# Self-attention on one core: order of the reciprocals, of the next norm's work and of the negated maxima

## Chip, core, metric

One core of a Trainium2 chip runs the whole program; seven cores are idle. The metric is the device time of one execution in microseconds (us). A core has TensorE (PE, matrix products into PSUM), VectorE (DVE), ScalarE (ACT), GpSimd (POOL, which reads and writes SBUF only) and SyncE (SP, which issues the DMAs). Each engine works through its own instructions in the order in which they are written and waits on semaphores for the others.

## The reference, cut to what matters

x is (8, 512, 256), the context (8, 64, 192), all float32. Two blocks follow each other: a cross-attention block (16 heads of 16, then a feed-forward), and a block of three parts. The first of these three is the self-attention that the change touches:

```python
def _ln(x, g, b):
    m = jnp.mean(x, axis=-1, keepdims=True)
    v = jnp.var(x, axis=-1, keepdims=True)
    return (x - m) * jax.lax.rsqrt(v + EPS) * g + b

# HEADS = 16, D_HEAD = 64, N = S = 512
q = (xq @ Wq).reshape(B, N, HEADS, D_HEAD)
k = (xc @ Wk).reshape(B, S, HEADS, D_HEAD)
v = (xc @ Wv).reshape(B, S, HEADS, D_HEAD)
attn = softmax(einsum('bnhd,bshd->bhns', q, k) * D_HEAD ** -0.5)
out = einsum('bhns,bshd->bnhd', attn, v).reshape(B, N, HEADS * D_HEAD)
return out @ Wo + bo

x = _attn(_ln(x, g1, b1), _ln(x, g1, b1), Wq1, Wk1, Wv1, Wo1, bo1) + x   # changed here
x = _attn(_ln(x, g2, b2), context, Wq2, Wk2, Wv2, Wo2, bo2) + x
x = _geglu_ff(_ln(x, g3, b3), Wp, bp, Wf, bf) + x
```

## The kernel before, in words

Precision is kept by splitting a float32 matrix in two: `hi`, a copy rounded to TensorE's fast type, and `lo`, the rest (value minus `hi`), rounded too. A product is then three matmuls, hi*hi + hi*lo + lo*hi (`mm3`, L146 to L148). The helpers that make the parts are `act_copy` (L156), `pool_copy` (L159), `dve_rest` (L162) and `pool_rest` (L165), and all their uses stand under these lines in the profile.

The self-attention stage (lines 1120 to 1595) is a pipeline over 64 units. A unit is one pair of heads of one batch; eight units make a batch (`b, p = divmod(s, 8)`, p is the position in it). In pass s of the loop every engine works on three units at once: the scores and exponentials of t = s, the projections and the maxima of u = s + 1, the weighted values of d = s - 1; normalising and output product come later still. Each pass has four quarters j = 0 to 3, one for each 128 keys. The order within a pass is written out by hand for each engine:

- TensorE, `pe_attention1`. Quarter 0: scores (L1268, then with the negated maximum L1272), query projection, values, key projection. Quarter 1: value projection. In quarters 1 to 3 the four products from which the maxima are taken (`largest`, L1305), and at the end of quarter 3 the transposes of the maxima (L152). The second score product of the next unit's quarter 0 waits for the negated maxima (`nm3_neg`); its first values product waits until ScalarE has copied the last sums and outputs out of PSUM (`d3_out`). For each second unit the output product is done in two halves: in quarter 3 of an odd pass (s odd), and in quarter 1 of the following even pass.
- ScalarE, `act_attention1`. Copies of the projections, exponentials (L1411), two of the four hi copies of the probabilities; in quarter 3 two copies of row sums into OB, two of outputs into OA, two of the negated maxima into `qb`, all with L156.
- VectorE, `dve_attention1`. Rests of queries (L1467) and keys (L1471) and of values, four rests of the probabilities (`rests`, L162, 128x1024; the one of quarter 3 is done at the head of the next pass), four maxima (L1496), the reciprocals of the sums (L1511), and the residual add of the output product (L1539), which stands in quarter 1 of even passes, in quarter 3 of odd ones.
- GpSimd, `pool_attention1`. In quarter 0 copies of the keys and of quarter 0's probabilities; then, in the order of its queue, OA times the spread reciprocals RS3 (L1577), hi and lo of that product; then quarter 3's probabilities.
- SyncE, `sp_attention1`. The row sums go from one partition each to 64 by two DMAs (L1233, L1234). After the reciprocal they go to memory (L1224) and come back spread over the partitions into RS3 (L1228).

The next batch's norm is made inside the stage. In the pass of position 4 VectorE takes the statistics (L239, L243, L246) at the end of quarter 0, GpSimd then raises the variance to the power -1/2 (L256), at the end of the pass VectorE scales (L262) and GpSimd adds the bias to the residual (L283). In position 6 TensorE transposes the scaled tile, ScalarE applies gain and bias, and GpSimd splits it in hi and lo.

Of the kernel before, what the change touches and what calls it, by code (L numbers as in the profile page):

```python
# [110 lines left out]
def build(nc, x, ctx_in, par, con, bias, wts, out):  # L111
    es = ExitStack()
    with es:  # L113
# [24 lines left out]
        pe, act, dve = Engine(nc.tensor), Engine(nc.scalar), Engine(nc.vector)  # L138
# [3 lines left out]
        def bank(i, n=1):  # L142
            return PS[:, 512 * i:512 * (i + n)]
# [11 lines left out]
        def act_copy(o, i, **k):  # L155
            return nc.scalar.activation(o, i, ACT.Identity, **k)  # L156
# [217 lines left out]
        def ok(v, n):  # L374
            return 0 <= v < n
# [29 lines left out]
        with nc.sbuf_tensor("R3", [128, 24576], FR) as r, nc.sbuf_tensor("F3", [128, NALL - 24576], FP) as g:  # L405
# [8 lines left out]
            OA, OB = wk[:, 2048:2560], wk[:, 2560:3072]  # L414
# [707 lines left out]
        N3 = 8 * NB  # L1122
# [72 lines left out]
        def tail3(s, j):  # L1195

            return 4 * (s - (N3 - 1)) + j - 1
# [191 lines left out]
        def act_attention1():  # L1389
            def project_q(u, h):  # L1390
                i, src = u % 2, bank(2)
                act.wait_ge(qk_mm, 2 * u)
                act.wait_ge(c3_mm, 4 * (u - 2) + 3)
                act_copy(qa[i][h][top, :], src[64 * h:64 * h + 64, :])
                act_copy(qa[i][h][low, :], src[64 * h:64 * h + 64, :]).then_inc(q3_hi.sem, 1)

            def project_k(u):
                act.wait_ge(qk_mm, 2 * u + 1)
                for h in range(2):
                    act_copy(ka[u % 2][h][top, :], bank(3)[64 * h:64 * h + 64, :]).then_inc(k3_hi.sem, 1)  # L1400

            def rounded(t, j):
                act.wait_ge(e3, 4 * t + j)
                act.wait_ge(d3_mm, 4 * (t - 1) + j)
                act_copy(P3[0][:, j, :], pst3[j % 2]).then_inc(p3_act.sem, 1)

            def exponent(t, j):
                n = 4 * t + j
                act.wait_ge(c3_mm, n)
                act.wait_ge(p3_lo, n - 2)  # L1410
                nc.scalar.activation(pst3[n % 2], bank(0, 2), ACT.Exp, scale=0.125).then_inc(e3.sem, 1)  # L1411

            ahead = act_attention2()
            for s in loop3:
                t, u, d = s, s + 1, s - 1
                b, p = divmod(max(t, 0), 8)
                for j in range(4):
                    if ok(u, N3) and j == 0:
                        project_q(u, 0)
                    if ok(t, N3):  # L1420
                        exponent(t, j)
                    if ok(u, N3) and j == 0:
                        project_q(u, 1)
                        project_k(u)
                    if ok(u, N3) and j == 1:
                        g = u // 2
                        act.wait_ge(v3_mm, u)
                        act.wait_ge(d3_mm, 4 * (2 * g - 3) + 3)
                        act.wait_ge(v3_set, 0)
                        src = bank(6).rearrange("p (t a e) -> p t a e", t=2, a=2)  # L1430
                        tt = slice(2 * (u % 2), 2 * (u % 2) + 2)
                        for c in range(2):
                            m = act_copy(v3_s[g % 2][0][:, tt, :, 128 * c:128 * c + 64], src[:, :, :, 64 * c:64 * c + 64])
                        m.then_inc(v3_hi.sem, 1)
                    if ok(t, N3) and j in (1, 2):
                        rounded(t, j)
                    if ok(d, N3) and j == 3:
                        act.wait_ge(d3_mm, 4 * d + 3)
                        act.wait_ge(sum3[(d - 1) % 2], 2 * ((d - 1) // 2) + 1)
                        wait_weights(act, "o1")  # L1440
                        act_copy(OB[64:65, :], bank(4)[64:65, :])
                        act_copy(OB[0:1, :], bank(5)[0:1, :]).then_inc(d3_sum.sem, 1)
                        act.wait_ge(o3_lo, d - 1)
                        act_copy(OA[0:64, :], bank(4)[0:64, :])
                        act_copy(OA[64:128, :], bank(5)[64:128, :]).then_inc(d3_out.sem, 1)
                    if ok(u, N3) and j == 3:
                        act.wait_ge(nm3_mm, u)
                        act.wait_ge(c3_mm, 4 * (u - 2) + 3)
                        act.wait_ge(k3_clear, u % 2)
                        for h in range(2):  # L1450
                            m = act_copy(qb[u % 2][h][64:65, :], bank(6)[64 * h:64 * h + 1, :], scale=-1.0)
                        m.then_inc(nm3_neg.sem, 1)
                    for _ in range(early4.get(tail3(s, j), 0)):
                        next(ahead)
                    if j == 2 and ok(t, N3) and p == 6:
                        ln_affine(18 + b, *((P_G1, P_B1) if b + 1 < NB else (P_G2, P_B2)), 6)
            for _ in ahead:
                pass

        def dve_attention1():  # L1460
# [39 lines left out]
            for s in loop3:  # L1500
                t, u, d = s, s + 1, s - 1
                b, p = divmod(max(t, 0), 8)
                more = ok(t, N3)
                for j in range(4):
                    if ok(u, N3) and j == 0:
                        project(u, 0)
                    if ok(d - 1, N3) and j == 0:
                        k, i = (d - 1) % 2, (d - 1) // 2
                        dve.wait_ge(sum3[k], 2 * i + 1)
                        dve.wait_ge(out3[k], i - 1)  # L1510
                        nc.vector.reciprocal(SR3[k], SQ3[k]).then_inc(rec3.sem, 1)  # L1511
                    if j == 0:
                        rests(4 * s - 1)
                    if ok(u, N3) and j == 0:
                        project(u, 1)
                        if u < 2:
                            clear(u)
                    if ok(u, N3) and j == 1:
                        s_ = v3_s[(u // 2) % 2]
                        src = bank(6).rearrange("p (t a e) -> p t a e", t=2, a=2)  # L1520
                        tt = slice(2 * (u % 2), 2 * (u % 2) + 2)
                        dve.wait_ge(v3_hi, u)
                        for c in range(2):
                            cs = slice(128 * c, 128 * c + 64)
                            m = dve_rest(s_[1][:, tt, :, cs], src[:, :, :, 64 * c:64 * c + 64], s_[0][:, tt, :, cs])
                        m.then_inc(v3_lo.sem, 1)
                    if ok(u, N3) and j >= 2:
                        largest(u, 2 * j - 3, 6)
                    e = s - 2 if j == 3 else s - 3
                    if j in (1, 2) or j == 3 and not (ok(e, N3) and e % 2 == 1):  # L1530
                        rests(4 * s + j - 1)
                    if j % 2 == 1 and ok(e, N3) and e % 2 == 1:
                        half = int(j == 1)
                        xv = xbuf(2, e // 8)[:, 2 * half:2 * half + 2, :]
                        dve.wait_ge(o3_mm, e - 1 + half)
                        dve.wait_ge(x_bias, 16 + e // 8)
                        if e % 8 > 1:
                            dve.wait_ge(o3_add, e - 3 + half)
                        nc.vector.tensor_tensor(xv, bank(out3_bank(e, half)).rearrange("p (a c) -> p a c", a=2), xv, ALU.add  # L1539
                                                ).then_inc(o3_add.sem, 1)  # L1540
                        if j == 3:
                            rests(4 * s + 2)
                    if ok(u, N3) and j in (1, 2):
                        largest(u, 2 * j - 2, 2)
                    if s == 0:
                        for job in g4[2 * j:2 * j + 2]:
                            dve_weight(job)
                    for _ in range(early4.get(tail3(s, j), 0)):
                        next(ahead)
                    if more and j == 0 and p == 4:  # L1550
                        ln_x_stats(*after3(b))
                if more and p == 4:
                    ln_scale(18 + b, xbuf(*after3(b)), C)
            for _ in ahead:
                pass
# [1 line left out]
        def pool_attention1():  # L1557
# [6 lines left out]
            for s in loop3:  # L1564
# [3 lines left out]
                for j in range(4):  # L1568
# [23 lines left out]
                    if j == 2 and more and p == 6:  # L1592
                        pool.wait_ge(v3_mm, 8 * (b - 1) + 7)
                        ln_split_pool(18 + b, ns[(b + 1) % 2])
                    if more and j == 0 and p == 4:
                        ln_pool_rstd(18 + b)
                if more and p == 4:
                    ln_add(pool, *after3(b))
            for _ in ahead:
                pass  # L1600
# [411 lines left out]
```

## Time and profile before

| | before |
|---|---|
| median of 3 runs | 2365.33 us (2363.18 to 2367.06) |
| profiled execution, its own time | 2370.57 us |
| its span | 2368.8 us |
| busy PE, DVE, ACT, POOL | 91%, 69%, 61%, 47% |
| granted TensorE clock, mean | 0.96 |

The profile is one execution. A row of a view in order of time has the start in us from the span's start, the duration in us, engine, line, operation, output<-input and a count where like instructions that follow each other are merged; in brackets stands how long the engine had been idle before it, and which engine, output and line ended that. A matmul's recorded duration overlaps the next one's, so starts are the thing to compare.

### The profile page before, as it was taken

The numbers are of one execution on the slowest core, as the hardware profiler recorded it, in microseconds if no ns is written. First come the engines' busy times: TensorE is split into PE (matmuls) and PEld (weight loads), VectorE is DVE, ScalarE is ACT, GpSimd is POOL, SyncE is SP. The second block draws the span as 40 slices with busy tenths as digits, with TensorE's granted clock in tenths as the row PEclk, the third lists the DMA queues.
The fourth block names the chain that finished last, engine by engine and source line by source line (L and its number), as shares of the span: only waits on it lengthen the run. The fifth ranks groups of instructions, "written<-read, shape, count | busy, mean of one in ns | idle before, by whom it ended". The sixth has DMA issues, their size and how long they took to land. (4 is left out here: it accounts for less than half of the span.)

```text
span 2368.8 us, 31297 instructions
## 1 busy us (share of the span) xinstructions
PE 2152.7 (91%) x11628; PEld 1792.3 (76%) x11628; DVE 1638.5 (69%) x2359; ACT 1439.6 (61%) x2082; POOL 1123.1 (47%) x877
## 2 busy tenths in 40 slices
PE   6867999998699999999999999999998789999998
PEld 4656788787477777877777787777777678999887
DVE  6566667665677777777777777777776776666554
ACT  5445566643377777777777777776775344555431
POOL 2145445545245444454544544545444566566432
PEclk8977999999799999999999999999999899999999
DMA  6710000011000000100001001000012521111000
GB/s 219 272 39 7 21 21 21 10 45 47 27 24 14 23 23 15 32 15 22 29 14 32 15 15 37 15 24 23 14 35 90 179 68 54 54 54 41 14 10 19
DMA packets 84280, 102.67 MB, mean 43 GB/s; under 512 B 29664, under 2 KB 61152, under 8 KB 83616
## 3 DMA queue, kind: packets, MB, share of 16 engines
q1 hardware_dynamic: 84128, 100.66, 12.8%
q8 instruction: 93, 1.52, 0.3%
q14 instruction: 59, 0.48, 0.1%
HBM read 65.50 MB, written 33.82 MB: 42 GB/s over the span
## 5 line engine op out<-in xcount | busy, mean ns | idle before, releaser
L146 PE MATMUL PS<-R 128*128 128x512 f32 (+1 forms) x2944 | 1034.5, 351 | 91.7 <-DVE R L162 50.4
L147 PE MATMUL PS<-R 128*128 128x512 f32 (+1 forms) x2944 | 1004.5, 341 | 0.0
L148 PE MATMUL PS<-R 128*128 128x512 f32 (+1 forms) x2944 | 1003.9, 341 | 0.0
L146 PEld LDWEIGHTS PS<-R 128*128 128x128 f32 x2944 | 570.4, 194 | 205.9 <-DVE R L162 64.1
L156 ACT ACTIVATE R<-PS 64x512 fp32r<-64x512 f32 (+4 forms) x860 | 460.4, 548 | 308.4 <-PE PS L1684 132.2
L148 PEld LDWEIGHTS PS<-R 128*128 128x128 f32 x2944 | 570.2, 194 | 62.4
L147 PEld LDWEIGHTS PS<-R 128*128 128x128 f32 x2944 | 571.8, 194 | 55.9
L162 DVE TENSOR_TENSOR R<-F,R 128x1024 fp32r<-128x1024 f32 (+2 forms) x410 | 482.1, 1179 | 54.0 <-POOL R L159 32.5
L159 POOL TENSOR_SCALAR R<-F 128x1024 fp32r<-128x1024 f32 (+1 forms) x359 | 308.5, 862 | 367.5 <-DVE F L1837 149.5
L1411 ACT ACTIVATE F<-PS 128x1024 f32<-128x1024 f32 x256 | 262.9, 1027 | 185.5 <-DVE R L162 141.4
L159 POOL TENSOR_SCALAR R<-R 64x512 fp32r<-64x512 f32 x128 | 142.7, 1128 | 395.8 <-ACT R L156 395.8
L162 DVE TENSOR_TENSOR R<-PS,R 128x512 fp32r<-128x512 f32 (+3 forms) x348 | 181.7, 543 | 191.4 <-ACT R L156 190.8
L1496 DVE TENSOR_REDUCE F<-PS 128x2 f32<-128x1024 f32 x256 | 301.8, 1216 | 8.4 <-PE PS L1305 8.3
L165 POOL TENSOR_TENSOR R<-F,R 128x512 fp32r<-128x512 f32 (+2 forms) x132 | 240.8, 1827 | 58.6 <-ACT R L156 39.3
L1467 DVE TENSOR_TENSOR R<-PS,R 64x512 fp32r<-64x512 f32 x128 | 88.0, 688 | 239.9 <-ACT R L156 239.9
L156 ACT ACTIVATE R<-F 128x1024 fp32r<-128x1024 f32 (+2 forms) x174 | 157.4, 920 | 66.4 <-PE PS L148 66.1
L1305 PE MATMUL PS<-R 128*128 128x512 f32 x512 | 167.8, 410 | 30.2 <-DVE F L1539 14.8
L156 ACT ACTIVATE F<-PS 64x512 f32<-64x512 f32 (+3 forms) x280 | 160.1, 593 | 48.7 <-PE PS L148 41.7
L1272 PE MATMUL PS<-R 128*128 128x512 f32 x512 | 164.0, 402 | 12.1 <-ACT R L156 11.5
L1268 PE MATMUL PS<-R 128*128 128x512 f32 x512 | 167.5, 408 | 1.4 <-ACT F L1411 1.4
L1305 PEld LDWEIGHTS PS<-R 128*128 128x128 f32 x512 | 88.9, 193 | 69.2 <-issue 31.7
L1577 POOL TENSOR_TENSOR F<-F 128x512 f32<-128x512 f32 x64 | 88.0, 1375 | 110.8 <-DMA F<-sd 110.8
(90 smaller groups left out, 1984.5 us busy)
## 6 DMA issues: line engine op xcount, KB each, us to landing
F<-sd SPq DMA_DIRECT2D x128, 128.0 KB, 2.9
xs<-F SPq DMA_DIRECT2D x16, 512.0 KB, 2.6
F<-xs SPq DMA_DIRECT2D x16, 512.0 KB, 3.5
gd<-F SPq DMA_DIRECT2D x8, 768.0 KB, 3.6
vd<-F SPq DMA_DIRECT2D x8, 768.0 KB, 5.7
R<-gd SPq DMA_DIRECT2D x6, 1024.0 KB, 5.7
R<-vd SPq DMA_DIRECT2D x6, 1024.0 KB, 5.6
F<-in_x SPq DMA_DIRECT2D x8, 512.0 KB, 5.1
```

Of the source, the lines that this page charges most:

```text
L146: nc.tensor.matmul(o, L[0], Rr[0], start=start, stop=False, skip_group_check=share)
L147: nc.tensor.matmul(o, L[0], Rr[1], start=False, stop=False, skip_group_check=share)
L148: return nc.tensor.matmul(o, L[1], Rr[0], start=False, stop=stop, skip_group_check=share)
L156: return nc.scalar.activation(o, i, ACT.Identity, **k)
L159: return nc.gpsimd.tensor_scalar(o, i, 1.0, 1.0, ALU.mult, ALU.mult)
L162: return nc.vector.tensor_tensor(o, i, f32(hi), ALU.subtract)
L165: return nc.gpsimd.tensor_tensor(o, i, f32(hi), ALU.subtract)
L1268: nc.tensor.matmul(bank(h), ka[i][h][:, kk], qa[i][h], start=True, stop=False)
L1272: m = nc.tensor.matmul(bank(h), kb[i][h][:, kk], qb[i][h], start=False, stop=True)
L1305: m = nc.tensor.matmul(bank(b0 + h), qa[i][h][:, 128 * q:128 * q + 128], ka[i][h], start=True, stop=True)
L1411: nc.scalar.activation(pst3[n % 2], bank(0, 2), ACT.Exp, scale=0.125).then_inc(e3.sem, 1)
L1496: nc.vector.tensor_reduce(M3[:, q, 0:128:64], bank(b0, 2).rearrange("p (a b) -> p a b", a=2), AX.X, ALU.max).then_inc(b3_max.sem, 1)
```

## The change

The reciprocals of VectorE move ahead of the query's rests in quarter 0. The two output copies of ScalarE become a function `summed`, called at its old place in odd passes and behind the negated maxima in even ones. The norm's statistics move from quarter 0 to quarter 3 of position 4, GpSimd's power to quarter 0 of position 5, and scaling and bias to the end of position 5. No instruction is added or taken away.

```diff
--- before.py
+++ after.py
@@ -1399,6 +1399,11 @@
                 for h in range(2):
                     act_copy(ka[u % 2][h][top, :], bank(3)[64 * h:64 * h + 64, :]).then_inc(k3_hi.sem, 1)
 
+            def summed(d):
+                act.wait_ge(o3_lo, d - 1)
+                act_copy(OA[0:64, :], bank(4)[0:64, :])
+                act_copy(OA[64:128, :], bank(5)[64:128, :]).then_inc(d3_out.sem, 1)
+
             def rounded(t, j):
                 act.wait_ge(e3, 4 * t + j)
                 act.wait_ge(d3_mm, 4 * (t - 1) + j)
@@ -1440,9 +1445,8 @@
                         wait_weights(act, "o1")
                         act_copy(OB[64:65, :], bank(4)[64:65, :])
                         act_copy(OB[0:1, :], bank(5)[0:1, :]).then_inc(d3_sum.sem, 1)
-                        act.wait_ge(o3_lo, d - 1)
-                        act_copy(OA[0:64, :], bank(4)[0:64, :])
-                        act_copy(OA[64:128, :], bank(5)[64:128, :]).then_inc(d3_out.sem, 1)
+                        if s % 2 == 1:
+                            summed(d)
                     if ok(u, N3) and j == 3:
                         act.wait_ge(nm3_mm, u)
                         act.wait_ge(c3_mm, 4 * (u - 2) + 3)
@@ -1450,6 +1454,8 @@
                         for h in range(2):
                             m = act_copy(qb[u % 2][h][64:65, :], bank(6)[64 * h:64 * h + 1, :], scale=-1.0)
                         m.then_inc(nm3_neg.sem, 1)
+                    if ok(d, N3) and j == 3 and s % 2 == 0:
+                        summed(d)
                     for _ in range(early4.get(tail3(s, j), 0)):
                         next(ahead)
                     if j == 2 and ok(t, N3) and p == 6:
@@ -1502,13 +1508,13 @@
                 b, p = divmod(max(t, 0), 8)
                 more = ok(t, N3)
                 for j in range(4):
-                    if ok(u, N3) and j == 0:
-                        project(u, 0)
                     if ok(d - 1, N3) and j == 0:
                         k, i = (d - 1) % 2, (d - 1) // 2
                         dve.wait_ge(sum3[k], 2 * i + 1)
                         dve.wait_ge(out3[k], i - 1)
                         nc.vector.reciprocal(SR3[k], SQ3[k]).then_inc(rec3.sem, 1)
+                    if ok(u, N3) and j == 0:
+                        project(u, 0)
                     if j == 0:
                         rests(4 * s - 1)
                     if ok(u, N3) and j == 0:
@@ -1547,9 +1553,9 @@
                             dve_weight(job)
                     for _ in range(early4.get(tail3(s, j), 0)):
                         next(ahead)
-                    if more and j == 0 and p == 4:
+                    if more and j == 3 and p == 4:
                         ln_x_stats(*after3(b))
-                if more and p == 4:
+                if more and p == 5:
                     ln_scale(18 + b, xbuf(*after3(b)), C)
             for _ in ahead:
                 pass
@@ -1592,9 +1598,9 @@
                     if j == 2 and more and p == 6:
                         pool.wait_ge(v3_mm, 8 * (b - 1) + 7)
                         ln_split_pool(18 + b, ns[(b + 1) % 2])
-                    if more and j == 0 and p == 4:
+                    if more and j == 0 and p == 5:
                         ln_pool_rstd(18 + b)
-                if more and p == 4:
+                if more and p == 5:
                     ln_add(pool, *after3(b))
             for _ in ahead:
                 pass
```

## Rows read from the trace of the kernel before

**Rows 1.** TensorE in order of time, units 32 and 33.
```profile
1225.30 0.71 PE L1268 MATMUL PS<-R 128*128 128x512 f32 x2
...
1237.31 0.70 PE L1305 MATMUL PS<-R 128*128 128x512 f32 x2
...
1243.56 0.66 PE L152 MATMUL PS<-F 128*128 128x128 f32 x4 [1.00 <-DVE F L1496]
1243.97 0.71 PE L1268 MATMUL PS<-R 128*128 128x512 f32 x2
...
1261.63 0.71 PE L1268 MATMUL PS<-R 128*128 128x512 f32 x2
```
**Rows 2.** TensorE's weight loads in order of time, end of unit 33.
```profile
1259.74 0.19 PEld L146 LDWEIGHTS PS<-R 128*128 128x128 f32 x1 [0.42 <-DVE F L1496]
```
**Rows 3.** DMA issues of the stage: the sums, with KB each, median us to landing.
```profile
F<-F SPq DMA_DIRECT2D x126, 2.0 KB, 1.8
```
**Rows 4.** VectorE in order of time, units 32 and 33.
```profile
1231.69 0.19 DVE L1511 RECIPROCAL F<-F 128x8 f32<-128x8 f32 x1
1231.80 1.17 DVE L162 TENSOR_TENSOR R<-F,R 128x1024 fp32r<-128x1024 f32 x1
...
1235.35 1.22 DVE L162 TENSOR_TENSOR R<-F,R 128x1024 fp32r<-128x1024 f32 x1
1236.48 0.68 DVE L1539 TENSOR_TENSOR F<-PS,F 128x512 f32<-128x512 f32 x1
...
1239.34 1.90 DVE L162 TENSOR_TENSOR R<-F,R 128x1024 fp32r<-128x1024 f32 x1
...
1253.87 1.22 DVE L162 TENSOR_TENSOR R<-F,R 128x1024 fp32r<-128x1024 f32 x1
...
1257.27 1.21 DVE L162 TENSOR_TENSOR R<-F,R 128x1024 fp32r<-128x1024 f32 x1
```
**Rows 5.** GpSimd in order of time, units 32 and 33.
```profile
1231.74 2.30 POOL L159 TENSOR_SCALAR R<-R 64x512 fp32r<-64x512 f32 x2 [7.13 <-ACT R L156]
1234.00 1.05 POOL L159 TENSOR_SCALAR R<-F 128x1024 fp32r<-128x1024 f32 x1
1236.79 1.29 POOL L1577 TENSOR_TENSOR F<-F 128x512 f32<-128x512 f32 x1 [1.74 <-DMA F<-sd]
...
1238.87 1.29 POOL L165 TENSOR_TENSOR R<-F,R 128x512 fp32r<-128x512 f32 x1
...
1252.53 1.05 POOL L159 TENSOR_SCALAR R<-F 128x1024 fp32r<-128x1024 f32 x1
...
1257.32 2.31 POOL L165 TENSOR_TENSOR R<-F,R 128x512 fp32r<-128x512 f32 x1
```
**Rows 6.** GpSimd and VectorE in order of time, pass 63.
```profile
1816.98 1.29 POOL L1577 TENSOR_TENSOR F<-F 128x512 f32<-128x512 f32 x1 [2.31 <-DMA F<-sd]
...
1817.21 2.13 DVE L162 TENSOR_TENSOR R<-F,R 128x1024 fp32r<-128x1024 f32 x1 [1.29 <-ACT R L156]
```
**Rows 7.** ScalarE in order of time, end of unit 32.
```profile
1242.59 2.27 ACT L156 ACTIVATE F<-PS 1x512 f32<-1x512 f32 x4 [0.23 <-PE PS L148]
```
**Rows 8.** TensorE in order of time, units 36 and 37.
```profile
1297.98 0.71 PE L1268 MATMUL PS<-R 128*128 128x512 f32 x2
...
1311.83 0.89 PE L1305 MATMUL PS<-R 128*128 128x512 f32 x2 [1.84 <-DVE F L1539]
...
1319.03 0.71 PE L1268 MATMUL PS<-R 128*128 128x512 f32 x2
...
1337.73 0.71 PE L1268 MATMUL PS<-R 128*128 128x512 f32 x2
```
**Rows 9.** VectorE and GpSimd in order of time, unit 36.
```profile
1307.13 1.41 DVE L239 BATCH_NORM_STATS2 F<-F 128x6 f32<-128x256 f32 x4
...
1308.99 0.17 DVE L246 TENSOR_SCALAR F<-F 128x4 f32<-128x4 f32 x1
...
1310.23 1.97 POOL L1577 TENSOR_TENSOR F<-F 128x512 f32<-128x512 f32 x1
```

## The prediction

> **What bounds the kernel now.** I read the page's busy shares first, then who waited for whom inside the self-attention stage, then one pair of units in order of time, engine by engine. The stage runs from about 609 to 1870 us of the span: 64 units (one head pair of one batch each, eight units to a batch) of 17.7 to 21.1 us, and all three edits lie there. TensorE is nearly full, but what opens its gaps is VectorE: in the view of waits ScalarE's exponentials wait for VectorE's rounding rests more than for anything else, and in order of time VectorE runs one unbroken chain in the middle of each unit. I take units 32 (even) and 33 (odd). Unit 32 starts when TensorE starts the scores at 1225.30, unit 33 at 1243.97, unit 34 at 1261.63: 18.67 and 17.66 us [rows 1]. In the even unit the chain ends at the transposes of the maxima, for which TensorE idles 1.00 us [rows 1]; in the odd unit it ends at the output product, whose weights wait 0.42 us for a maximum [rows 2].
>
> I call quarter j=0's rounding rest `rest0`, quarter 1's `rest1`; `multiply` is GpSimd's OA*RS3.
>
> **Reciprocal first.** The sums' DMA lands 1.8 us after its issue [rows 3], about 1.7 us into a unit, while VectorE is just done with the rest of the unit before. The reciprocal can then run some 4.5 us earlier and nothing waits behind it. What follows it, from its own row, starts 0.11 us earlier (1231.69 instead of 1231.80) [rows 4]: -0.11 us on the chain of every unit. It also sends the two DMAs earlier. From the reciprocal's end (1231.88) to the multiply's start (1236.79) are 4.9 us [rows 4, 5], so RS3 is now there 7 to 8 us into the unit, and the multiply, which sat idle 1.74 us for that DMA, no longer waits: it starts on the heels of GpSimd's copy of quarter 0. That copy ends at 1235.05, and a GpSimd instruction that waits for nothing starts 0.04 us before its predecessor's recorded end (1231.74 + 2.30 against 1234.00) [rows 5].
>
> There it meets VectorE's rest0. The copy's end, less 0.11, puts the multiply at 1234.90 and rest0 at 1235.24: the multiply is 0.34 us ahead. In unit 33 the same sum gives 1253.43 and 1253.76, 0.33 us [rows 4, 5]. This kernel shows what then happens, once, on operations of these very shapes: at 1816.98 the multiply started 0.23 us before a rest, and the rest took 2.13 us instead of 1.17 [rows 6]. VectorE stood until the multiply was nearly done. With 1.2 us less the head start I take +0.86 us. Bounds: 0 if VectorE gets through, 1.29 (a whole multiply).
>
> In the even unit this is partly paid back. rest1 there takes 1.90 us instead of 1.21, because GpSimd's rest at 1238.87 started 0.47 us ahead of it; with the multiply 1.9 us earlier that GpSimd rest is over before rest1 starts: -0.69. In the odd unit there is nothing to win: rest1 was 0.05 us ahead and lost nothing (1.21), GpSimd's rest took the wait (2.31) [rows 4, 5].
> Even unit, VectorE's chain: -0.11 + 0.86 - 0.69 = +0.06. But its residual add, between the two, comes at +0.75, and TensorE waits for exactly that (the add ends at 1237.16, the next pair of products starts at 1237.31) [rows 1, 4]. So TensorE reaches the end of the values 0.75 later, which its 1.00 us wait at the transposes hides from TensorE itself.
>
> The Trainium skill, "SBUF — State Buffer", section "Who interferes with whom", says that a VectorE instruction with two SBUF inputs contends with a GpSimd instruction that reads SBUF, and that the one issued first keeps the port while the other blocks entirely. By that rule the multiply wins, which is the forecast; were it the other way, the sum would be the second rival's. The pair at 1816.98 agrees with 2.13 us. At 1231.74 GpSimd is on record 0.06 us ahead of VectorE's 1231.80 and is still the one that waits (2.30 us for two copies) [rows 4, 5], so a head start must be more than that; 0.34 is.
>
> **Negated maxima ahead of outputs in even units.** No instruction is added. ScalarE's block at the unit's end is four copies in 2.27 us from 1242.59 (two of sums, two of outputs), and then the two negations [rows 7], after which it copies the next unit's first query half; none waits for the one before. The negations come 1.2 us earlier, the outputs 1.2 us later. TensorE in the odd unit used to wait for the negations (some 0.3 us, more behind the norm's unit), and now waits right behind, at the first values product, for the outputs. The end of the block doesn't move by the swap, and VectorE's next chain hangs on what comes after it. So I cost the swap at 0 to the unit; bounds: -0.46 us in odd units (two score products that can now run in the wait), +0.55 if ScalarE must stand for the transposes between the sums and the negations. What does move it is that the block starts with the values' end, which is now 0.75 later. The odd unit's chain therefore starts 0.75 later, 0.69 relative to its unit.
> Odd unit: 0.69 - 0.11 + 0.86 = +1.44, all of it on the wait in [rows 2].
>
> **Statistics and scaling.** In the fifth unit of a batch four statistics (1.41 us) and their aggregation, 2.0 us in all from 1307.13 to 1309.16, stand in the middle of VectorE's chain, and TensorE idles 1.84 us for the add behind them [rows 8, 9]. The fifth unit takes 21.05 us in this batch (1297.98 to 1319.03), the sixth 18.70 [rows 8]. Counted the same way, the fifth unit takes 21.1 us in three of the eight batches (this one is the second of them) and 20.1 in the other five, mean 20.5; the sixth has a mean of 18.4. Moved to the end, the statistics lie in VectorE's gap at the head of the next unit, as the scaling did, and the scaling goes to the same gap one unit later; the transposes that need it come some 10 us after. GpSimd's power now stands before the multiply in the sixth unit: there rest0 goes first, the multiply is held (as it was here, 1.97 us at 1310.23 [rows 9]), and GpSimd's last rest lands about 0.3 us ahead of rest1: +0.9 on rest1 in place of rest0. Price of the move itself: fifth unit 20.5 to 18.7, and the sixth's excess over 17.7 goes: 2.5 us a batch gained, 20 us in all.
>
> **Sum** for a batch of eight. Positions 0 and 2: +0.06 each. 1 and 3: +1.44 each. 4: 18.73 - 20.5 = -1.8. 5: 17.7 + 0.69 - 0.11 + 0.9 = 19.2 against 18.4, +0.8. 6: a norm's unit, in which TensorE carries the late add straight to its end, -0.11 + 0.86 = +0.75. 7: -0.11 + 0.86 = +0.75 (its start hangs on the values' end before and after, so nothing is added). Total +3.5 us, 8 batches: +28. I take +25, since the first and last units lack parts of the pattern. The profiled execution (2370.57 us, span 2368.8) is 5.2 us above the median 2365.33; the difference is laid on the median: **2390 us**. Its own range is 2377 to 2402, from 0.65 to 1.0 us of growth in rest0.
>
> **Rivals.**
> 1. The norm's relief decides and the early multiply costs little. For it: 2.0 us of statistics do leave the chain of every fifth unit [rows 9], and the swap and the reciprocal each can only shorten a wait. Against: the rows around rest0 touch each other without a gap up to the maxima. In the growth g of rest0 the batch is about 10g - 5 us: two pairs at 3g - 1.1, the rest by the same steps. It turns at g = 0.5. With g near 0.2, or the multiply left where it was: -15 to -20, 2345 to 2350 us. Take 2348.
> 2. VectorE goes first and the multiply is held till rest0's end. Then GpSimd's last rest lands 0.3 us ahead of the odd unit's rest1 and that grows by 0.9: a pair +0.9 (the even one -0.5, ScalarE standing +0.55), positions 4 and 5 -1.7, position 7 +0.8; batch +0.7, +6 us: 2371. Against it: the row at 1816.98.
> 3. The swap pays its full stall. For it: TensorE's waits for the negations; against: the outputs stand right behind. 32 x 0.46 = 15 us less than the forecast: 2375.
> That the multiply isn't early at all (DMAs late) has the same time as rival 1, and the 4.9 us speak against it.
>
> **How the numbers follow.** Forecast 0.56, rival 1 0.27, rival 2 0.10, rival 3 0.07. A difference under 0.2% (4.7 us) can't be told from none. Rivals 2 (6 us) and 3 (10 us) lie just above that, so of their 0.17 I put 0.07 within it: faster 0.27, same 0.07, slower 0.56 + 0.10 = 0.66. The range goes from 2346, to take in most of rival 1, to 2402.
>
> **What would show it.** In the changed profile: GpSimd's multiply with next to no idle time for its DMA; rest0 at about 2.0 us where it was 1.2, in six or seven of eight units, and rest1 in even units at 1.2 instead of 1.9; odd units of 19 us and fifth units of 18.7; TensorE waiting for the residual add in even units (0.9 us instead of 0.2) and for the maximum before the output product in odd ones. Wrong: rest0 at 1.2 us throughout, or odd units at 17.7.

## The result, and the profile after

| | before | after |
|---|---|---|
| median, same chip | 2366.19 us (2363.18 to 2368.61) | 2406.03 us (2398.02 to 2407.41, 4 runs) |
| ratio, with its 95% interval | | 1.0158 [1.0138, 1.0178] |
| profiled execution, its own time; span | 2370.57; 2368.8 us | 2404.77; 2402.9 us |
| granted TensorE clock, mean | 0.96 | 0.96 |

The change makes the kernel 1.6% slower: +39.8 us by the medians, +34.1 by the spans. The direction and the collision were forecast, the size (+25) was too small, and the time lies 4 us above the range. The granted clock is the same in both, 0.96 over the span and 0.99 in the self-attention stage. VectorE's busy time grew most, from 1638.5 to 1679.7 us with the same instructions, and GpSimd's from 1123.1 to 1151.5: that is waiting inside instructions and not work. The page's busy times of after:

```profile
PE 2161.9 (90%) x11628; PEld 1786.9 (74%) x11628; DVE 1679.7 (70%) x2359; ACT 1443.6 (60%) x2082; POOL 1151.5 (48%) x877
```

The table to read is the unit's length by its position in the batch: start of a unit's scores to start of the next one's (as in [rows 1]), mean over units 6 to 61, seven for each position, us.

| position | 0 | 1 | 2 | 3 | 4 | 5 | 6 | 7 | sum |
|---|---|---|---|---|---|---|---|---|---|
| before | 18.68 | 17.72 | 18.77 | 17.73 | 20.52 | 18.40 | 19.42 | 18.75 | 149.99 |
| after | 18.76 | 19.18 | 18.76 | 19.16 | 18.70 | 20.12 | 20.20 | 19.54 | 154.42 |
| difference | +0.08 | +1.46 | -0.01 | +1.43 | -1.82 | +1.72 | +0.78 | +0.79 | +4.43 |
| predicted | +0.06 | +1.44 | +0.06 | +1.44 | -1.8 | +0.8 | +0.75 | +0.75 | +3.5 |

Eight batches of 4.43 are 35.4 us, the growth of the span within 1.3. All positions but one came within 0.07 us of the forecast; position 5 grew by twice its own.

VectorE of after in order of time. Unit 32: the last quarter's rest of the unit before, rest0, residual add, rest1. Unit 33: reciprocal, rest0, rest1. Last row: rest0 of unit 37, a position 5:

```profile
1250.01 1.21 DVE L162 TENSOR_TENSOR R<-F,R 128x1024 fp32r<-128x1024 f32 x1
...
1253.60 2.04 DVE L162 TENSOR_TENSOR R<-F,R 128x1024 fp32r<-128x1024 f32 x1
1255.56 0.68 DVE L1545 TENSOR_TENSOR F<-PS,F 128x512 f32<-128x512 f32 x1
...
1258.43 1.21 DVE L162 TENSOR_TENSOR R<-F,R 128x1024 fp32r<-128x1024 f32 x1
...
1265.23 0.20 DVE L1515 RECIPROCAL F<-F 128x8 f32<-128x8 f32 x1 [2.20 <-DMA F<-F]
...
1273.03 2.05 DVE L162 TENSOR_TENSOR R<-F,R 128x1024 fp32r<-128x1024 f32 x1
...
1277.27 1.21 DVE L162 TENSOR_TENSOR R<-F,R 128x1024 fp32r<-128x1024 f32 x1
...
1348.89 3.03 DVE L162 TENSOR_TENSOR R<-F,R 128x1024 fp32r<-128x1024 f32 x1
```

GpSimd of after in the same stretches. Unit 32: copy of quarter 0, multiply, hi, lo. Unit 33: multiply. Unit 37: power and multiply:

```profile
1252.26 1.04 POOL L159 TENSOR_SCALAR R<-F 128x1024 fp32r<-128x1024 f32 x1
1253.27 1.28 POOL L1583 TENSOR_TENSOR F<-F 128x512 f32<-128x512 f32 x1
1254.64 1.47 POOL L159 TENSOR_SCALAR R<-F 128x512 fp32r<-128x512 f32 x1
1256.20 1.29 POOL L165 TENSOR_TENSOR R<-F,R 128x512 fp32r<-128x512 f32 x1
...
1272.71 1.28 POOL L1583 TENSOR_TENSOR F<-F 128x512 f32<-128x512 f32 x1
...
1348.56 1.02 POOL L256 TENSOR_TENSOR F<-F 128x4 f32<-128x4 f32 x1
1349.55 1.29 POOL L1583 TENSOR_TENSOR F<-F 128x512 f32<-128x512 f32 x1
```

The reciprocal now runs 2.9 us into unit 33 (1265.23; the unit starts at 1262.37, below), where it ran 6.2 us into it in before; in unit 32 it went from 6.4 to 1.8. The multiply no longer has idle time before it: it starts 0.33 and 0.32 us ahead of rest0 (1253.27 against 1253.60, and 1272.71 against 1273.03), and rest0 takes 2.04 and 2.05 us where it took 1.22 [rows 4]. GpSimd pays too: its hi copy at 1254.64 takes 1.47 us and ends behind rest0, where the same copy takes 0.6 in nearly every unit of before. rest1 of the even unit is back to 1.21 from 1.90. In unit 37 the power starts 0.33 us ahead of rest0 and the multiply stands right behind it, and rest0 takes 3.03 us: it is held until the multiply, too, is nearly done.

TensorE of after in order of time shows what the 0.8 us do further on:

```profile
1243.62 0.48 PE L1268 MATMUL PS<-R 128*128 128x512 f32 x1
...
1256.39 0.47 PE L1305 MATMUL PS<-R 128*128 128x512 f32 x1 [0.77 <-DVE F L1545]
...
1261.96 0.66 PE L152 MATMUL PS<-F 128*128 128x128 f32 x4 [0.31 <-DVE F L1502]
1262.37 0.48 PE L1268 MATMUL PS<-R 128*128 128x512 f32 x1
...
1281.56 0.71 PE L1268 MATMUL PS<-R 128*128 128x512 f32 x2
```

Even unit: TensorE waits for the late residual add (0.77 us at 1256.39) and in return only 0.31 us for the transposes instead of 1.00 [rows 1]. Its length is 1262.37 - 1243.62 = 18.75. The unit after it takes 19.19 where it took 17.66. In the view of waits, for 1243 to 1543 us (total, times, longest), the add's wait comes once in each pair of units, at nearly the same length:

```profile
PE PS L1305 <- DVE F L1545: 6.1, 8, 0.8
```

ScalarE's block at the end of the even unit has the new order, sums, negations, outputs; in order of time:

```profile
1261.69 1.19 ACT L156 ACTIVATE F<-PS 1x512 f32<-1x512 f32 x2 [0.78 <-PE PS L148]
1262.90 1.18 ACT L156 ACTIVATE R<-PS 1x512 fp32r<-1x512 f32 x2
1264.11 1.19 ACT L156 ACTIVATE F<-PS 64x512 f32<-64x512 f32 x2
```

It starts 18.07 us into the unit (1261.69 - 1243.62), where it started 17.29 in before (1242.59 - 1225.30, [rows 7, 1]): +0.78, the late add handed on.

### The profile page after: what moved, and what is told of

It is laid out like the page before. It is cut to its first block and busy times, and to the rows that moved or that the text cites. A ratio compares the mean times of both kernels' runs of the same rounds, so it can differ in the third digit from the quotient of the medians.

```text
span 2402.9 us, 31297 instructions
## 1 busy us (share of the span) xinstructions
PE 2161.9 (90%) x11628; PEld 1786.9 (74%) x11628; DVE 1679.7 (70%) x2359; ACT 1443.6 (60%) x2082; POOL 1151.5 (48%) x877
## 5 line engine op out<-in xcount | busy, mean ns | idle before, releaser
L159 POOL TENSOR_SCALAR R<-F 128x1024 fp32r<-128x1024 f32 (+1 forms) x359 | 374.3, 1045 | 498.3 <-PE PS L148 196.3
L162 DVE TENSOR_TENSOR R<-F,R 128x1024 fp32r<-128x1024 f32 (+2 forms) x410 | 521.4, 1275 | 53.6 <-POOL R L159 32.2
L165 POOL TENSOR_TENSOR R<-F,R 128x512 fp32r<-128x512 f32 (+2 forms) x132 | 212.2, 1610 | 58.7 <-ACT R L156 39.4
L1843 DVE SCALAR_TENSOR_TENSOR F<-PS,F 128x512 f32<-128x512 f32 x64 | 47.8, 748 | 103.8 <-PE PS L148 59.9
```

The lines of the kernel that those rows point to most:

```text
L159: return nc.gpsimd.tensor_scalar(o, i, 1.0, 1.0, ALU.mult, ALU.mult)
L162: return nc.vector.tensor_tensor(o, i, f32(hi), ALU.subtract)
L165: return nc.gpsimd.tensor_tensor(o, i, f32(hi), ALU.subtract)
```

## The experiments

All times are medians; the kernel before ran beside each group at 2362 to 2369 us, and each ratio is against it. Lists by position are means over units 6 to 61, as in the table above. A name in bold is a kernel.

### The three edits, each alone

**e1_recip** is before with the reciprocal moved:

```diff
                 for j in range(4):
-                    if ok(u, N3) and j == 0:
-                        project(u, 0)
                     if ok(d - 1, N3) and j == 0:
                         ...
                         nc.vector.reciprocal(SR3[k], SQ3[k]).then_inc(rec3.sem, 1)
+                    if ok(u, N3) and j == 0:
+                        project(u, 0)
```

> The kernel before with the reciprocals moved, nothing else. Theory A (the early multiply takes the port ahead of quarter 0's rest): rest0 about 2.05 us in positions 0 to 3 and 5 to 7, odd units at 19.1; position 4, where power and multiply stood before, unchanged; batch 2 x (0.06 + 1.44) + 3 x 0.75 = +5.3 us, 8 batches +42, about 2408. Rival B (the reciprocal costs nothing by itself, the loss comes from the moved power or the swap): rest0 1.2 us, about -7 us, 2359.

Measured 2394.81 us, ratio 1.0123 [1.0096, 1.0151]. VectorE's rest0 in order of time, unit 33:

```profile
1264.17 2.05 DVE L162 TENSOR_TENSOR R<-F,R 128x1024 fp32r<-128x1024 f32 x1
```

So this edit alone brings 27 us, and with rest0 at 2.05 the place is the predicted one; the 42 that I expected were too many. By positions: 18.76 19.04 18.76 19.04 20.05 18.74 20.19 19.41, which is +4.0 a batch and not +5.3. Positions 1 and 3 grew by 1.32 instead of 1.44, position 5 by 0.34 instead of 0.75, and position 4 fell by 0.47: it takes about 20.05 us in every batch, where three batches of before had 21.1. In position 4 the four statistics still stand in the chain, but the power, which follows them, starts 0.62 us ahead of the next rest and the multiply only behind it, and the rest goes first; GpSimd and VectorE of unit 36:

```profile
1321.69 1.02 POOL L256 TENSOR_TENSOR F<-F 128x4 f32<-128x4 f32 x1 [1.50 <-DVE F L246]
1322.68 1.98 POOL L1577 TENSOR_TENSOR F<-F 128x512 f32<-128x512 f32 x1
```

```profile
1322.31 1.22 DVE L162 TENSOR_TENSOR R<-F,R 128x1024 fp32r<-128x1024 f32 x1
```

**e2_norm** is before with the norm's four moves alone:

```diff
-                    if more and j == 0 and p == 4:
+                    if more and j == 3 and p == 4:
                         ln_x_stats(*after3(b))
-                if more and p == 4:
+                if more and p == 5:
                     ln_scale(18 + b, xbuf(*after3(b)), C)
 ...
-                    if more and j == 0 and p == 4:
+                    if more and j == 0 and p == 5:
                         ln_pool_rstd(18 + b)
-                if more and p == 4:
+                if more and p == 5:
                     ln_add(pool, *after3(b))
```

> The kernel before with statistics, power, scaling and bias moved, nothing else. Theory A: position 4 falls from 20.5 to 18.7 and position 5 keeps or loses little; the power alone, 0.32 us ahead of quarter 0's rest, holds the port by itself for up to its 1.0 us (rest0 +0.7 in position 5) or, if it only held in company with the multiply behind it, not at all: -14 to -20 us, 2346 to 2352. Rival B (the moved norm is what costs): above 2366.

Measured 2344.96 us, ratio 0.9909 [0.9881, 0.9938]: some -22 us, 1 us better than the range I expected. Position 4 fell from 20.52 to 18.69 and position 5 from 18.40 to 17.76, 2.5 us a batch as computed. GpSimd and VectorE, unit 37:

```profile
1319.52 1.01 POOL L256 TENSOR_TENSOR F<-F 128x4 f32<-128x4 f32 x1
...
1321.29 1.28 POOL L1577 TENSOR_TENSOR F<-F 128x512 f32<-128x512 f32 x1 [0.76 <-DMA F<-sd]
```

```profile
1319.84 1.22 DVE L162 TENSOR_TENSOR R<-F,R 128x1024 fp32r<-128x1024 f32 x1
```

The power is 0.32 us ahead of rest0, as in after, and rest0 loses nothing: 1.22 us. What differs from after's 3.03 is that the multiply does not follow at once; e4_held, below, changes nothing but that.

**e3_negated** is before with the swap alone (`summed` behind the negations where `s % 2 == 0`).

> The kernel before with the outputs' copies behind the negations in even passes, nothing else. Theory A: ScalarE stands for the transposes between sums and negations in positions 0 and 2, 0.5 us, so odd units get up to 0.5 us longer there: 0 to +8 us, 2366 to 2374. Rival C (the swap pays its stall): odd units 0.3 to 0.5 us shorter, 2351 to 2356. Rival B (the swap is the cause of the loss): 2390 or more.

Measured 2373.57 us, ratio 1.0033 [1.0017, 1.0048]: +6 us. Odd units grew from 17.72 to 18.25 (positions 1 and 3), position 5 not (18.36 against 18.40). I take it that there the norm set the end: without the norm (e10_norm_swap) position 5 pays as well. ScalarE in order of time, end of an even unit:

```profile
1244.22 1.19 ACT L156 ACTIVATE F<-PS 1x512 f32<-1x512 f32 x2 [0.31 <-PE PS L148]
1245.80 1.18 ACT L156 ACTIVATE R<-PS 1x512 fp32r<-1x512 f32 x2 [0.40 <-PE PS L152]
1247.01 1.19 ACT L156 ACTIVATE F<-PS 64x512 f32<-64x512 f32 x2
```

ScalarE stands 0.40 us for the transposes between sums and negations, with the outputs queued behind. In before the outputs filled that time. In after this wait is gone (the row at 1262.90 has none), because the block starts later. There the swap costs little: positions 1 and 3 take 19.18 and 19.16 us in after and 19.04 in e1_recip, so swap and moved norm together add at most 0.14. No run is after without the swap.

### The collision taken away

**e4_held** is after with one wait on GpSimd, so that the multiply starts only when rest0 is done:

```diff
                     if ok(d - 1, N3) and j == 0:
                         f = d - 1
+                        if more:
+                            pool.wait_ge(p3_lo, 4 * t)
                         pool.wait_ge(in3[f % 2], 2 * (f // 2) + 1)
```

> The changed kernel, in which GpSimd waits before the multiply until VectorE has finished quarter 0's rest. Theory A: rest0 back to 1.2 us in all units; the multiply then starts 0.1 us after that rest, and GpSimd's own rest comes 2.1 us after it: in odd units about level with rest1, in even ones 0.7 us ahead (+0.5). Odd units 17.7 to 18.5, about 2345 to 2360. Rival B (the port is not the cause): rest0 shorter but the time stays at 2400 or so.

Measured 2358.50 us, ratio 0.9965 [0.9948, 0.9982], inside the expected range. VectorE's rest0 and GpSimd's multiply in unit 33:

```profile
1278.22 1.21 DVE L162 TENSOR_TENSOR R<-F,R 128x1024 fp32r<-128x1024 f32 x1
```

```profile
1279.52 1.30 POOL L1585 TENSOR_TENSOR F<-F 128x512 f32<-128x512 f32 x1 [1.60 <-DVE R L162]
```

One wait on an engine with half its time free gives back 47 us, all of the loss and more. This is the test that settles the cause: same order on VectorE and ScalarE, only the two starts are apart. By positions: 18.47 18.17 18.51 18.18 18.47 18.63 19.36 18.79. It settles position 5 as well. In unit 37 the power is still 0.33 us ahead of rest0, but the multiply no longer follows, and rest0 takes 1.22 us instead of 3.03 (GpSimd, then VectorE):

```profile
1314.54 1.01 POOL L256 TENSOR_TENSOR F<-F 128x4 f32<-128x4 f32 x1
```

```profile
1314.87 1.22 DVE L162 TENSOR_TENSOR R<-F,R 128x1024 fp32r<-128x1024 f32 x1
```

**e9_recip_held** is e1_recip with the same wait.

> The kernel before with the reciprocals first and the multiply held back until quarter 0's rest is done; norm and copies as before. Theory A (all of the early reciprocal's cost is the port at quarter 0's rest): the 27 us it cost alone go, 2355 to 2370. Rival (the early DMAs or the reciprocal's place cost something themselves): 2375 or more.

Measured 2353.10 us, ratio 0.9948 [0.9925, 0.9970]. So the early reciprocal is worth some -14 us (-12 by the positions) if the multiply does not meet rest0, and costs 27 if it does. Nearly half of the gain is in position 5, 17.76 instead of 18.40, which is also where e2_norm gains. VectorE in an even unit, rest0 and rest1, and the two of the odd one:

```profile
1226.44 1.21 DVE L162 TENSOR_TENSOR R<-F,R 128x1024 fp32r<-128x1024 f32 x1
...
1230.44 1.75 DVE L162 TENSOR_TENSOR R<-F,R 128x1024 fp32r<-128x1024 f32 x1
...
1244.91 1.22 DVE L162 TENSOR_TENSOR R<-F,R 128x1024 fp32r<-128x1024 f32 x1
...
1248.31 1.22 DVE L162 TENSOR_TENSOR R<-F,R 128x1024 fp32r<-128x1024 f32 x1
```

rest0 is at 1.2 in both; position 0 takes 18.47 us instead of 18.68. rest1 of the even unit is still held (1.75 us). GpSimd, odd unit:

```profile
1246.21 1.29 POOL L1579 TENSOR_TENSOR F<-F 128x512 f32<-128x512 f32 x1 [1.59 <-DVE R L162]
...
1248.30 2.38 POOL L165 TENSOR_TENSOR R<-F,R 128x512 fp32r<-128x512 f32 x1
```

The multiply starts behind rest0 and the GpSimd rest at 1248.30, with VectorE's at 1248.31, is the one that waits (2.38).

### Position 5

**e5_power_early** is after with the power at the end of position 4 instead of in quarter 0 of position 5, so that GpSimd has only the multiply at rest0:

```diff
-                    if more and j == 0 and p == 5:
-                        ln_pool_rstd(18 + b)
+                if more and p == 4:
+                    ln_pool_rstd(18 + b)
```

> The changed kernel with GpSimd's power of the next norm at the end of position 4 instead of in position 5, so that no power stands between the copy of quarter 0 and the multiply. Theory A (in position 5 power and multiply hold the port one behind the other, 3.03 us for rest0): rest0 of position 5 falls to 2.05 us as in the other units, position 5 from 20.15 to 19.2, 8 us less in all, about 2398 against 2406. Rival (position 5 is long because of the statistics ahead of it): 20.1 stays.

Measured 2396.58 us, ratio 1.0130 [1.0109, 1.0151]; position 5 is 19.15 instead of 20.12, and no other position moved by more than 0.02. Unit 37, VectorE and GpSimd:

```profile
1343.44 2.06 DVE L162 TENSOR_TENSOR R<-F,R 128x1024 fp32r<-128x1024 f32 x1
```

```profile
1343.12 1.30 POOL L1583 TENSOR_TENSOR F<-F 128x512 f32<-128x512 f32 x1
```

2.06 instead of 3.03: the further microsecond goes with the power. 0.97 by 8 batches is 7.8 us, and the medians differ by 9.4.

**e8_norm_power** is e2_norm with that same edit, which asks whether the power costs anything without a multiply behind it.

> The kernel before with the norm's work moved and the power at the end of position 4, neither reciprocals nor copies touched. Theory A: the power alone did not cost anything in position 5 (17.76 us there, against 17.72 in positions 1 and 3), so this stays at 2345, within 3 us. Rival (the power alone holds the port too): 5 us less.

Measured 2348.59 us, ratio 0.9927 [0.9912, 0.9942], against e2_norm's 0.9909 [0.9881, 0.9938] (3.6 us apart by medians from different groups of runs): no difference that can be told. Positions 4 and 5 are 18.69 and 17.76 in both. Alone, the power is free.

### Another way round the collision

**e6_order** and **e7_order_no_swap** (the same without the swap) leave the starts free and change GpSimd's queue in quarter 0: the probabilities' copy and the multiply ahead of the copies of the keys; the power at the end of position 4.

```diff
+                    if ok(t, N3) and j == 0:
+                        pool.wait_ge(e3, 4 * t + j)
+                        pool.wait_ge(d3_mm, 4 * (t - 1) + j)
+                        pool_copy(P3[0][:, j, :], pst3[j % 2]).then_inc(p3_pool.sem, 1)
+                    if ok(d - 1, N3) and j == 0:
+                        ...
+                        nc.gpsimd.tensor_tensor(OA, OA, RS3, ALU.mult).then_inc(mul3.sem, 1)
                     ... copies of the keys, then hi and lo of the product
```

> The changed kernel with GpSimd's queue in another order: in quarter 0 first the copy of the probabilities, then the multiply, then the copies of the keys (needed only a pass later); hi and lo of the product at their old place; the power at the end of position 4. Theory A: the multiply is over before rest0 starts, and the product's rest before rest1: both 1.2 us in every unit. Even units 0.3 to 0.7 us shorter than before, odd ones 0.4 longer by the swap: 2335 to 2350. Rival (early reciprocals cost through something other than the port): 2375 or more.

> As the run before it, but with ScalarE's copies in the order of the kernel before. Theory A: the swap costs 6 us by itself, so this is the faster of the two by about 5 us, 2330 to 2345, and faster than the kernel with the norm moved alone (2345). Rival (the swap pays once VectorE's chain is shorter): slower than the run before it.

Measured 2370.36 us, 1.0014 [0.9999, 1.0028], and 2367.50 us, 0.9993 [0.9979, 1.0008]. Both are outside what I expected. Even units did fall, to 18.0 us (17.95 and 18.14 in e6_order, 18.00 in e7_order_no_swap), but odd units rose to 18.6 to 18.9, and a pair takes 36.8 to 37.0 against 36.4 to 36.5 in before, which eats what the norm gives. ScalarE and VectorE of e7_order_no_swap, whose units start at 1222.65, 1240.59 and 1259.20:

```profile
1239.89 2.28 ACT L156 ACTIVATE F<-PS 1x512 f32<-1x512 f32 x4 [0.78 <-PE PS L148]
```

```profile
1251.10 1.62 DVE L162 TENSOR_TENSOR R<-F,R 128x1024 fp32r<-128x1024 f32 x1
```

The block starts 17.24 us into the even unit, as in before (17.29). TensorE's transposes come earlier, so the next unit is said to start earlier, but what paces its chain, ScalarE's block and the query copies behind it, has not moved: the even unit's gain is the odd one's loss. That was an error in how I read a unit's length. A residual collision is left too: rest0 in the odd unit takes 1.62, with a GpSimd copy 0.07 us ahead of it:

```profile
1251.03 0.63 POOL L159 TENSOR_SCALAR R<-F 128x512 fp32r<-128x512 f32 x1
```

### What the parts give together

**e10_norm_swap** is before with the norm's moves and the swap, no reciprocal.

> The kernel before with the norm's work moved and the copies swapped, reciprocals as before, so that only the reciprocals' place parts it from the changed kernel. Theory A: norm and swap add up, -22 + 6: 2351, so the reciprocals cost 55 us in this company against 27 alone, the difference in position 5, where power and multiply hold the port together. Rival (norm and swap disturb each other): 2365 or more.

Measured 2361.97 us, ratio 0.9975 [0.9959, 0.9990], some 11 us above what I expected and nearer to the rival, in which the two disturb each other: with the norm out of the way position 5 pays for the swap too (18.30 against 17.76), so that the swap costs 0.52, 0.51 and 0.54 us in positions 1, 3 and 5, 12.6 us in all (the medians of e10_norm_swap and e2_norm, from different groups of runs, are 17 apart). The reciprocal's step is then 2406 - 2362 = 44 us in company, 27 alone. In company it brings position 5's double hold (18.30 to 20.12, alone 18.40 to 18.74) and has nothing to win in position 4 (alone -0.47), while it costs less in positions 1 and 3 (0.9 against 1.32).

**e11_best** is before with the early reciprocal, the norm's moves and the held multiply, but not the swap; **e12_best_power** also has the power at the end of position 4.

> The version the runs point to: reciprocals first, the norm's work moved, the multiply held back until quarter 0's rest is done, ScalarE's copies as before. Theory A: the norm's -22 us (positions 4 and 5, 2.5 us a batch) and the -12 us of the held early reciprocal lie in different units and add up: 2332 to 2336, faster than any kernel so far. In position 5 the power stands 0.3 us ahead of rest0 with no multiply at its heels, so rest0 stays at 1.2 us there. Rival (they get in each other's way in position 5): 2345.

> The run before it with the power at the end of position 4. In the run before, position 5 took 18.8 us in 6 of the 8 batches (17.75 in 2): GpSimd's rest of the product started 0.02 us ahead of rest1 there and rest1 took 2.36 us. Theory A (two starts a few hundredths of a us apart decide, and the power shifts GpSimd's or VectorE's by so little): without the power position 5 is as positions 1 and 3, 17.75, and the time is 6 us lower, about 2340. Rival (the statistics at the head of position 5 are the cause): 18.8 stays, 2347.

Measured 2346.97 us, 0.9929 [0.9905, 0.9954], and 2336.46 us, 0.9871 [0.9844, 0.9897]. The second beats both kernels: 29 us under before, 70 under after. The first missed its 2332 to 2336 by 11 us and came out where the rival (2345) put it. Part of the miss is that -22 and -14 do not add up: both edits take position 5 from 18.40 to 17.76, and that 0.64 us a batch can be won only once. The other part is a new collision in position 5. The two kernels differ at rest1 of position 5, of which VectorE's and GpSimd's rows stand below, first of e11_best (unit 45), then of e12_best_power (unit 37):

```profile
1467.98 2.36 DVE L162 TENSOR_TENSOR R<-F,R 128x1024 fp32r<-128x1024 f32 x1
```

```profile
1467.96 1.30 POOL L165 TENSOR_TENSOR R<-F,R 128x512 fp32r<-128x512 f32 x1
```

```profile
1315.75 1.22 DVE L162 TENSOR_TENSOR R<-F,R 128x1024 fp32r<-128x1024 f32 x1
```

```profile
1313.65 1.30 POOL L1579 TENSOR_TENSOR F<-F 128x512 f32<-128x512 f32 x1 [1.58 <-DVE R L162]
...
1315.74 2.37 POOL L165 TENSOR_TENSOR R<-F,R 128x512 fp32r<-128x512 f32 x1
```

The two rests start within 0.02 us of each other in both. In e11_best GpSimd wins and position 5 takes 18.8 us in six of eight batches; in e12_best_power VectorE wins in all eight and it takes 17.74. Why the tie falls differently these rows don't show. By positions that is 0.76 us a batch, 6 us; the medians are 10.5 apart, and the rest is not explained.

## Where the prediction held, and the step that failed

1. **The reciprocal frees the multiply, which meets rest0 (step right).** Predicted head start 0.34 and 0.33 us, recorded 0.33 and 0.32; predicted growth 0.86, recorded 0.82 and 0.83 (2.04 and 2.05 against 1.22). e1_recip shows it without the other edits, e4_held and e9_recip_held show that it is the cause. The rule of the Trainium skill ("SBUF — State Buffer", "Who interferes with whom") that the instruction issued first keeps the port agrees with these rows; rival 2, in which VectorE goes first, is out. The power does not follow that rule by itself: in e2_norm and e4_held it starts 0.32 and 0.33 us ahead of rest0, and rest0 takes 1.22 us.
2. **Even units hardly change, odd ones take it all (right, with some luck).** +0.08 and -0.01 for +0.06; +1.46 and +1.43 for +1.44. The agreement of the odd units is closer than the sum deserves: all of the 1.44 was put down to the reciprocal, which alone gives 1.32 (e1_recip), and 0.12 to 0.14 came with the swap and the norm, which had been costed at nothing there. The wait for the residual add grew by about the same 0.75 and the one for the transposes shrank, as worked out. At the output product of the odd unit, though, where I laid the whole +1.44, TensorE's weight load waits only this:

```profile
1279.67 0.19 PEld L146 LDWEIGHTS PS<-R 128*128 128x128 f32 x1 [0.31 <-DVE F L1502]
```

   The rest is taken earlier in the unit. TensorE in order of time, at the first values product and at one of the products for the maxima:

```profile
1265.45 0.47 PE L146 MATMUL PS<-R 128*128 128x512 f32 x1 [0.51 <-ACT F L156]
...
1276.27 0.74 PE L1305 MATMUL PS<-R 128*128 128x512 f32 x2 [0.57 <-DVE F L1502]
```

   So TensorE waits for ScalarE's late outputs, and then for a maximum. The unit's length came out as worked out, the place of the wait did not.
3. **The swap at nothing (nearly right in after, wrong alone).** In e3_negated and e10_norm_swap it costs +0.53 an odd unit, the upper bound that I had named and not taken (ScalarE standing for the transposes). In after the block starts 0.78 later, which covers that stall. With the multiply held the price is back: positions 1 and 3 take 18.17 us in e4_held and 17.75 in e11_best, which is the same kernel without the swap.
4. **The norm (right for position 4, wrong for position 5).** -1.82 for -1.8, and e2_norm gives -22 us for -20. The step that failed is "there rest0 goes first, the multiply is held (as it was here, 1.97 us at 1310.23 [rows 9])", costed at +0.9 on rest1. Recorded: power, then multiply, both served ahead of rest0, which takes 3.03 us, while rest1 keeps its 1.21. The term of +0.9 thus measured +1.8, and position 5 grew by 1.72 instead of 0.8; with the power taken away it is 0.97 us shorter (e5_power_early). I had drawn the order from a row of before in which the power was 0.62 us ahead and the rest went in between ([rows 9]; e1_recip's unit 36 is the same case), and applied it to a head start of 0.3. In before, unit 36, GpSimd and VectorE:

```profile
1309.24 1.02 POOL L256 TENSOR_TENSOR F<-F 128x4 f32<-128x4 f32 x1 [1.50 <-DVE F L246]
```

```profile
1309.86 1.21 DVE L162 TENSOR_TENSOR R<-F,R 128x1024 fp32r<-128x1024 f32 x1
```

5. **Positions 6 and 7 (right).** +0.78 and +0.79 for +0.75.
6. **From the sum to the time.** The forecast was +25 and the medians give +39.8. The difference of 14.8 is made of three parts. 7.4 come from the positions (4.43 against 3.5 a batch, nearly all position 5). 1.7 come from the first and last units, for which I took 3 off the sum of 28, while the traces show 1.3 (35.4 by positions, 34.1 by spans). The rest, 5.7, lies between spans and medians. The profiled execution of before was 4.4 us above its median and that of after 1.3 below, and I had laid a profile's difference on the median.

The range's upper end (growth of rest0 up to 1.0 us) varied that term alone: it had no room for an order of the two engines that I had read from one row. Without the 7 us of position 5 the time would have lain inside the range.

## What to carry to other kernels

Making an instruction of GpSimd ready earlier is not free, even where that engine is half idle: look up what VectorE starts within a microsecond of its new place, and hold GpSimd back by a wait on that instruction if they meet. Here that one wait turned +27 us into -14. Before calling a unit shorter, check that the block which paces the next one starts earlier as well; a start that moves alone only shifts time from one unit to its neighbour.

## What the runs showed that was not expected

- A power over 128x4 elements (1.02 us) that starts 0.32 us ahead of VectorE's rest costs it nothing when nothing follows (e2_norm: 1.22 us), and with a multiply at its heels the same rest takes 3.03 us (after). e4_held parts the two by nothing but the multiply's wait. At 0.62 us ahead, with the multiply behind it, VectorE still goes first (1.22, e1_recip, and [rows 9]). Why 0.32 and 0.62 differ stays open; no run varied that distance by itself.
- A rest that has lost ends a fixed time after the multiply, whatever stood before: 1.09 us in unit 32 (1253.60 + 2.04 against 1253.27 + 1.28), 1.08 in unit 37 (1348.89 + 3.03 against 1349.55 + 1.29), 1.07 for the pair of [rows 6] (1817.21 + 2.13 against 1816.98 + 1.29). As the rest takes 1.21 us when nothing holds it, it seems to start some 0.1 us before the multiply's end, an estimate from these rows.
- Recorded starts do not order the two engines below some 0.06 us: GpSimd 0.06 ahead and still waiting ([rows 4, 5]: 1231.74, 1231.80), 0.01 ahead and waiting (e12_best_power, 2.37 us), 0.02 ahead and winning (e11_best, VectorE 2.36 us). In e11_best's two other batches GpSimd is 0.02 ahead at the same place and waits (2.39 us in unit 13).
- The price of losing is large against the time in dispute: 1.1 us on a 1.2 us instruction for a difference of a hundredth in the start.
